# Exact softmax with a pass for the maxima against online softmax in blocks, in a cross-attention kernel

## The reference

```python
qh = (q @ wq + bq).reshape(b, -1, 16, 32).transpose(0, 2, 1, 3)     # 128 queries
kh = (k @ wk + bk).reshape(b, -1, 16, 32).transpose(0, 2, 1, 3)     # 2048 keys
vh = (v @ wv + bv).reshape(b, -1, 16, 32).transpose(0, 2, 1, 3)
score = softmax(einsum('bhqd,bhkd->bhqk', qh, kh) / 32 ** 0.5, axis=-1)
out = einsum('bhqk,bhkd->bhqd', score, vh)                          # then @ wo + bo, + x
```

## Time and profile before

| | |
|---|---|
| median of 3 runs | 3335.28 us (3335.01 to 3337.17) |
| profiled execution: span | 3332.6 us |
| TensorE busy | 3315.3 us |
| VectorE busy | 2431.5 us |
| GpSimd busy | 2110.4 us |
| ScalarE busy | 1300.5 us |
| TensorE items of this stage (line 101, two groups) | 770.9 and 743.7 us |

### The profile page before, as it was taken

The page is one execution under the profiler, slowest core; times in us unless marked ns, Lnnn a source line. Parts: engine busy times, 40 slices in busy tenths (PEclk is TensorE's granted clock), DMA queues, the critical chain, the costliest instruction groups (busy, mean ns, idle before and its releaser), DMA issues.

```text
span 3332.6 us, 81287 instructions
## 1 busy us (share of the span) xinstructions
PE 3315.3 (99%) x32145; PEld 2661.9 (80%) x32145; DVE 2431.5 (73%) x3790; ACT 1300.5 (39%) x1809; POOL 2110.4 (63%) x1537
## 2 busy tenths in 40 slices
PE   9999999999999999999999999999999999999999
PEld 6777777777777777777777777778888888888888
DVE  6566676666766766677676676767887688789997
ACT  3244444444444444444444444454213322321111
POOL 3277978879788798797987979862555000033332
PEclk9999999999999999999999999999999999999999
DMA  4111111111121111111111111122122423310000
GB/s 166 60 39 49 40 52 58 37 52 39 49 58 40 52 38 51 58 40 49 46 46 56 39 52 52 43 81 77 64 99 102 137 83 108 129 66 20 25 19 19
DMA packets 211351, 199.06 MB, mean 60 GB/s; under 512 B 11520, under 2 KB 168560, under 8 KB 209520
## 3 DMA queue, kind: packets, MB, share of 16 engines
q1 hardware_dynamic: 211056, 194.50, 18.5%
HBM read 156.32 MB, written 38.13 MB: 58 GB/s over the span
## 4 chain that ended last, share of the span: by engine, by line
PE 96%; DVE 3%; issue 0%; POOL 0%; ACT 0%; DMA 0%; SPq 0%; DVEq 0%; POOLq 0%
PE a_bank L101 70%; PE a_bank L1725 7%; PE a_bank L1697 7%; PE a_bank L1688 6%; PE a_bank L790 1%; PE a_bank L1677 1%; PE a_bank L2723 1%; PE a_bank L801 0%; PE a_bank L865 0%; PE a_bank L1713 0%; PE a_bank L1744 0%; PE a_bank L839 0%; PE a_bank L2696 0%; PE a_bank L1737 0%; PE a_bank L2219 0%
## 5 line engine op out<-in xcount | busy, mean ns | idle before, releaser
L1473 DVE TENSOR_REDUCE x_maxima<-a_bank 128x1 f32<-128x512 f32 x960 | 616.3, 684 | 331.0 <-PE a_bank L1688 331.0
L1344 ACT ACTIVATE x_probsT<-x_probsT 128x1024 f32<-128x1024 f32 x480 | 509.2, 1061 | 810.1 <-DVE x_probsT L1484 810.1
L101 PE MATMUL a_bank<-x_ctx,x_wk 128*128 128x512 f32 x3072 | 770.9, 400 | 0.0
L101 PE MATMUL a_bank<-x_wv,x_ctx 128*128 128x512 f32 x3072 | 743.7, 391 | 0.0
L101 PEld LDWEIGHTS a_bank<-x_ctx,x_wk 128*128 128x128 f32 x3072 | 557.7, 188 | 157.3 <-issue 32.6
L101 PEld LDWEIGHTS a_bank<-x_wv,x_ctx 128*128 128x128 f32 x3072 | 573.2, 188 | 130.4 <-ACT x_v L1326 5.4
L1484 DVE TENSOR_TENSOR x_probsT<-a_bank,x_shift_all 128x1024 f32<-128x1024 f32 x480 | 583.4, 1216 | 2.0 <-PE a_bank L1697 1.7
L1047 POOL TENSOR_TENSOR x_pairs<-x_probsT 128x1024 f32<-128x1024 f32 x240 | 576.7, 2403 | 12.9 <-ACT x_probsT L1344 10.8
L1238 POOL TENSOR_TENSOR x_ctx<-x_tile_raw,x_one 128x512 fp32r<-128x512 f32 x236 | 245.3, 1039 | 294.3 <-PE a_bank L101 292.7
L1510 DVE SCALAR_TENSOR_TENSOR x_k<-a_bank,x_bk,x_k 128x512 fp32r<-128x512 f32 x240 | 180.2, 751 | 305.7 <-ACT x_k L1333 305.7
L1240 POOL TENSOR_TENSOR x_ctx<-x_tile_raw,x_ctx 128x512 fp32r<-128x512 f32 x236 | 301.6, 1278 | 18.5
(11 more groups left out here) (224 smaller groups left out, 4458.1 us busy)
## 6 DMA issues: line engine op xcount, KB each, us to landing
x_tile_raw<-in_ctx SPq DMA_DIRECT2D x236, 256.0 KB, 3.1
x_shift_all<-shifts SPq DMA_DIRECT2D x60, 256.0 KB, 3.6
m_ff_src<-in_w_ff SPq DMA_DIRECT2D x44, 192.0 KB, 2.5
wq_ff<-m_ff_dst SPq DMA_DIRECT2D x44, 192.0 KB, 1.8
attT<-x_out SPq DMA_DIRECT2D x32, 256.0 KB, 2.0
s_attT<-attT SPq DMA_DIRECT2D x16, 512.0 KB, 4.2
m_w_raw<-in_w SPq DMA_DIRECT2D x32, 256.0 KB, 3.0
f_w_in<-wq_ff SPq DMA_DIRECT2D x22, 256.0 KB, 3.4
```

The source lines that it names most:

```text
L101: mm = pe.matmul(out, lhs[a], rhs[b], start=first and n == 0, stop=last and n == 2)
L1344: act.activation(half, half, ACT.Exp).then_inc(exped, 1)
L1473: dve.tensor_reduce(maxima[:, c, g * HG + j:g * HG + j + 1], banks[:, j], AX.X, ALU.max).then_inc(maxed, 1)
```

## The change

Softmax becomes online. The batch is cut into 8 blocks: 2 halves of the keys (8 tiles of 128) by 4 head groups; 128 blocks in all, counted through (`Block`, `run_blocks`: a loop body of 24 blocks). There is no `top`, no second computation of the scores and no maxima a batch ahead. Instead, for each block:

- TensorE computes the scores in two halves of 4 tiles; ScalarE copies each half out of banks 0 to 3 into one of three SBUF buffers (`keep_scores`, two copies of 1024 columns for each half).
- VectorE folds the 8 tiles of a block into one by a maximum over tiles (`fold`, twice, for two heads each); TensorE turns the four results (`turn_folds`), VectorE takes the maximum over the free axis (`shift_columns`), TensorE turns that into rows (`turn_shift`), ScalarE copies them (`keep_shift`), SP saves and loads them broadcast.
- One block later ScalarE puts the table of shifts into a PSUM bank (`make_table`), VectorE adds it to the scores in SBUF (`add_shift`, four times), ScalarE takes exp (twice 2048 columns). Two blocks later TensorE weights, three blocks later it sums the denominators (`sum_up`, one for each block). For the second half of the keys the sums so far are first scaled by exp of the drop of the maximum (`ease` on GpSimd).
- Items are made 3 blocks ahead, four in a block, all copied once (no low part of the keys is needed).

More of the change, by code:

```diff
@@ L318, with __init__, ahead, back @@
 UNROLL = 4
+PER_BATCH = 8
+RING = 3
+PERIOD = PER_BATCH * RING
+BLOCKS = B * PER_BATCH
+class Block:
+    def __init__(self, n, k):
+        self.n, self.k = n, k
+        self.group, self.half, self.at = k % HG, k % PER_BATCH // HG, k % PER_BATCH
+        self.turn = k // PER_BATCH
+    def ahead(self, d):
+        return Block(self.n + (self.k + d) // PERIOD, (self.k + d) % PERIOD)
+    def back(self, d):
+        return self.ahead(-d)
+    def count(self, per=1, plus=0):
+        return self.n * (PERIOD * per) + (self.k * per + plus)
+    def batch(self):
+        return self.n * RING + self.turn if isinstance(self.n, int) else None
+    def batches(self, per=1, plus=0):
+        return self.n * (RING * per) + (self.turn * per + plus)
+    def seconds(self, per=1, plus=0):
+        return self.n * (PERIOD // 2 * per) + ((self.turn * HG + self.group) * per + plus)
+    def ring(self):
+        return self.k % RING
+    def number(self):
+        return self.n * PERIOD + self.k if isinstance(self.n, int) else None
+    def exists(self):
+        return not isinstance(self.n, int) or 0 <= self.number() < BLOCKS
+    def from_end(self):
+        return self.number() - BLOCKS if isinstance(self.n, int) else -BLOCKS
+def run_blocks(nc, eng, step, until):
+    for k in range(PERIOD):
+        step(Block(0, k))
+    with looped(nc, eng, 1, BLOCKS // PERIOD) as n:
+        for k in range(PERIOD):
+            step(Block(n, k))
+    for k in range(BLOCKS // PERIOD * PERIOD, until):
+        step(Block(k // PERIOD, k % PERIOD))
 class Tile:
@@ L1458, in _ @@
+            for c in range(2):
+                late.weights_hi(act, 4, c)
             late.scalar(act)
@@ L1695, in score @@
+            def score(s, h):
+                c = 2 * s.half + h
+                g = s.group
+                if s.half == 0 and h == 0 and g % 2 == 0:
+                    pe.wait_ge(q_loaded[g // 2], START + s.batches(16, 16))
+                pe.wait_ge(k_ready, START + s.batches(KT, c * DC + g + 1))
+                if h:
+                    pe.wait_ge(kept, START + s.count(HG, 2))
+                elif s.back(1).exists():
+                    pe.wait_ge(kept, START + s.count(HG))
                 for t in range(TPC):
@@ L1810, in back, with weigh @@
[L1810 to L1814 removed]
+            def weigh(s, e):
+                pe.wait_ge(exped, START + e.count(2, 2))
+                if e.group == 0:
+                    pe.wait_ge(v_ready, START + e.batches(KT, BLOCK_TILES * (e.half + 1)))
+                last = s.back(1)
+                pe.wait_ge(shift_kept, START + (last.count(1, 1) if last.exists() else BLOCKS))
+                if last.half:
+                    pe.wait_ge(drop_kept, START + (last.seconds(1, 1) if last.exists() else B * HG))
+                if s.from_end() == -ITEMS_AHEAD:
+                    pe.wait_ge(k_ready, START + B * KT)
+                for t in range(BLOCK_TILES):
+                    for j in range(HG):
+                        mm = pe.matmul(bank[rows(j), misc_bank(s), 0:S],
+                                       v_t[:, e.half * BLOCK_TILES + t, cols(e.group * HG + j, DH)],
+                                       scores_of(e)[:, j, t], start=t == 0, stop=t == BLOCK_TILES - 1)
+                mm.then_inc(pv_done, 1)
@@ new lines, in _, with end_step, end_turns @@
+            for g in range(2):
+                pe.wait_ge(v_ready, START + g + 3)
+                key_item(Block(0, 2), g, 6 + g)
+            q.project(pe, 2)
+            q.turn(pe, 3)
+            for v in range(2):
+                pe.wait_ge(k_ready, START + v + 5)
+                value_item(Block(0, 2), v, 6 + v)
+            q.project(pe, 3)
+            run_blocks(nc, pe, step, BLOCKS - ITEMS_AHEAD)
+            def end_step(k):
+                step(Block(k // PERIOD, k % PERIOD))
+            def end_turns(k):
+                s = Block(k // PERIOD, k % PERIOD)
+                turn_folds(s)
+                turn_shift(s)
```

1226 lines of the change are left out of this document (482 added, 744 removed).

## The result

The changed kernel takes 4058.1 us (median of four runs, 4047.4 to 4070.4) against 3336.1 us (3335.0 to 3337.2) for the kernel before on the same chip: ratio 1.2165, 95% interval 1.2134 to 1.2195. The forecast was 3873 us with a range up to 4040: the right direction, and 185 us too little.

What follows compares the result with a forecast made beforehand. TensorE's own work bounds the kernel before; a block becomes 16.6 us of work plus 4.55 of waiting, against 17.17. Start 96, blocks 2644, last three 76 and rest 1053.6 give 3870, predicted 3873 us; range 3490 to 4040.

Steps and rivals of the forecast that it cites:

- granted clock at full: Sign expected in the profile after: TensorE's granted clock stays at full despite the two pauses in a block.
- The clock falls: Rival: work after TensorE's long pause runs at 1.2 GHz, 3.4 us more per block, 4300 us; one in eight, 50; chance 0.05.
- The wait before `turn_folds`: TensorE, free at 14.5 us in the block round, waits 3.0 us for two folds on VectorE ending at 17.5.
- The fold: VectorE's stepped maximum over 2048 elements: 3.75 us, between 2.29 (contiguous) and 4.35 (full element price).
- The wait before `weigh`: TensorE waits 1.5 us for the exponential's second half, which stands behind `keep_shift` on ScalarE.
- The moved key item: Key item ahead of score half 1 on TensorE: hides that half's wait for the first copies, and buys only this.
- The shifts through memory: Save and load of the shift row: first two `add_shift` end 2 us before the folds can start, costing nothing.
- Start and tail: Block 0 starts at 96 us; the last three blocks, without items, take 76 us.
- The rest of the kernel: After the blocks the kernel goes on as the kernel before does from 2279.0 us: 1053.6 us.
- The faster rival: TensorE hides both waits: round of 16.6 us, 3300 us in all, turning point at a round of 16.9; chance 0.06.
- The likeliest part of the range: Both waits with a fold of 3.2 to 4.35 us: 3740 to 4040 us, chance 0.71.
- the signs the prediction asked for: TensorE near 80% busy, fold 3.3 to 4.35 us, block 21 us, waits of 3 and 1.5 us, clock full.

Runs made afterwards that it cites:

- e2: Kernel as changed plus ten unneeded 512-column matmuls per block on TensorE, right before the wait of `turn_folds`; 3902.7 us.
- e7: Kernel as changed with `turn_folds` moved ahead of the second key item of a block on TensorE; 4470.4 us.
- e1: Kernel as changed with the two folds reading the same scores in storage order, so the output is not the reference's; 3498.6 us.
- e8: e4 plus the ten matmuls before the wait of `turn_folds`; 3878.7 us.
- e10: Kernel as changed with seven tile comparisons replacing the folds, second-half exponential ahead of `keep_shift`, and `add_shift` 3 ahead of `shift_columns`; 3308.4 us, ratio 0.9917 to the kernel before.
- e6: Kernel as changed with the second half of the scores put back ahead of the first key item, on TensorE alone; 4216.4 us.
- e11: e10 with the second half of the scores put back ahead of the first key item on TensorE; 3911.2 us.
- e12: e2 with the row of shifts loaded twice in sequence, the second load waiting for the first; 4218.5 us.
- e4: Kernel as changed with the exponential of the second half ahead of `keep_shift` on ScalarE; 3943.3 us.
- e5: e4 with `add_shift` 3 also moved ahead of `shift_columns` on VectorE; 3943.1 us.

## Why the prediction was right or wrong, point by point

The sum, term by term, against the profiled executions of the kernel as changed and of e2, in which the clock is nearly full:

| us | forecast | as changed | e2 |
|---|---|---|---|
| block 0 starts | 96 | 103.4 | 102.0 |
| blocks 0 to 124 | 2644 | 2775.8 | 2634.5 |
| last three blocks | 76 | 101.3 | 101.3 |
| from there to the end | 1053.6 | 1066.1 | 1066.1 |
| sum | 3870 | 4046.6 | 3903.9 |

- *The step that failed* is the term that the sum doesn't have: the forecast put the loss by the clock at nothing ("granted clock at full") and gave *The clock falls* a chance of 0.05. In the runs this term is 141 of the 177 us in the table, and 155 us by the medians of the kernel as changed and of e2 (the profiled execution lay 10 us below its median). I had the mechanism, its place and a price for one event, 3.4 us; the highest that the trace shows is 0.4 in the turns and 2.3 to 2.5 in the item, and the mean over all blocks 0.10 and 1.16. What was wrong above all is how often: "if one in eight did, 50". Of the 125 value items behind the turns 85 took 3.9 us or more, two in three. The only row on it spoke for a clock at the lower level, and no row spoke against; I had no row of TensorE pausing inside the loop, and took the absence for evidence. TensorE: Matmul & The Clock Gate of the Trainium skill, in HAM oscillation, describes a loop in which each wait starts the next work cold. The trace agrees in kind, with a granted clock of 0.942 and an item of 5.32 us in place of 3.01, but not in every round: 40 of the 125 items behind the pause kept their 3.0 us.
- *The wait before `turn_folds`*, 3.0 us: 3.10 measured. In the mean over the blocks the folds start 9.9 us after `turn_shift` (forecast 10.0) and end at 17.4 (17.35). Right, and e7 shows its working: 2.86 less work ahead of the turns gave 2.55 more of pause.
- *The fold*, 3.75 between 2.29 and 4.35: 3.81. The choice was right though its reason was thin, so the closeness is in part luck: the two prices it stood between, 3.3 and 4.35, have their middle at 3.83, not at 3.75. e1 settles what the prediction left open: the excess, 1.53 us for 2048 elements or 0.75 ns each, belongs to the step, since eight elements per output in storage order cost nothing more. The small-step rows of lines 1515 and 1522 had 1.0 ns of excess for each. The Vector Engine (DVE) Microarchitecture Reference of the Trainium skill, section 5.2, gives full rate for adjacent words and 1.73 ns per column for one hopping source, measured on programs with two sources. The trace agrees in kind: the fold's 3.81 us are 1.86 ns per column, e1's 2.28 us are 1.11, both with the fixed cost in them. The prediction says that this figure would put the time within 10 us of its own; by its own sums (3.67 for 3.75, two folds in each of 125 blocks) it is 20.
- *The wait before `weigh`*, 1.5 us: 1.67 in the block shown, 178 us in all, 1.4 a block. Right. That it stands behind `keep_shift` is right only in part: with the exponential first and a full clock (e8) 104 of 178 us stay, because `add_shift` 3 stands behind `shift_columns`. I had named only the first of two orders that hold it; it takes both (e10: 9 us).
- *The moved key item "buys only" a hidden copy*: wrong. In e6 the copy needed almost no hiding (0.15 us a block), and putting the item back costs 158 us through ScalarE's order; where comparisons stand there too the item's place is worth 603 us (e11).
- *The shifts through memory*, about 2 us spare: 1.84 us of idle time before the folds. Right, and e12 shows that what exceeds it is paid.
- *Start and tail* were 6 to 7 and 25 us too short, at either clock. At the start TensorE waited 3.82 us for `q_y` at 41.5, which I had not allowed for. In the tail I took each of the last blocks as a round without its items. But with no items TensorE waits 8.8, 8.8 and 15.2 us for folds and twice some 8 us for Pool's sum (kernel as changed):

```profile
2894.35 1.11 PE L1664 MATMUL a_bank<-x_id,x_folds 128*128 128x128 f32 x4 [8.81 <-DVE x_folds L1483]
...
2941.31 1.11 PE L1664 MATMUL a_bank<-x_id,x_folds 128*128 128x128 f32 x4 [15.23 <-DVE x_folds L1483]
...
2970.39 0.65 PE L1654 MATMUL a_bank<-x_total,x_ones 128*32 128x128 f32 x8 [8.31 <-POOL x_total L1275]
```

- *The rest of the kernel* takes 12 to 13 us more than in the kernel before, in the kernel as changed, in e2 and in e10. Its first 36 products take 10.9 us in e10 where they took 8.49; they too follow a pause. Behind them TensorE waits 8.6 us for VectorE's `s_phi_k` where it waited 0.3, and this is most of it.
- *The faster rival* had 3300 us at a round of 16.6, and its turning point against the kernel before at 16.9. e10 reaches 3308 us, but at a round of 16.34: start, tail and rest took 1267 us where the rival had 1220 for them. With them as measured the kernel before is matched at a round of about 16.5, not 16.9. And it takes another fold and two other orders than the change has.
- *The likeliest part of the range*: with a fold of 3.25 us the prediction names a round of 20.3 and 3760 us. By its own steps, 0.5 us less for each of two folds, it is 20.15 and 3750.
- Among the signs the prediction asked for, most came: a busy share of 80% in the middle (500 to 2500 us), the fold, both waits at their sizes, none elsewhere of note in the loop. The releaser before `weigh` is the exponential; before `turn_folds` the profile names a fold for 66 of 423 us and no releaser for 357. "Granted clock at full" failed, and a round of 21 us with it. With the clock restored (e2) the round is 21.14 us against 21.15.

## What to carry to other kernels

When a change puts a pause into a loop whose TensorE had none, price the clock with it: look at the item behind each pause, and set a case for it that covers most rounds, not one in eight. A cheap test is to fill the pause with products that nobody needs; if the kernel gets faster by more work and the granted clock comes back, it was the clock. A maximum over tiles read with a large step is better made as a running comparison of whole tiles, and a step moved on one engine must be moved in the order of the engine that consumes it. Removed waits don't add up while something slow lies beside them: the same reordering was worth 115 us beside a slow item and 24 us without it.

## What the runs showed of the hardware that I had not expected

- Pauses of 2.45 to 5.7 us in the loop were followed by transposes, scores or items that ran at 1.2 GHz for a part or all of their time. The item behind was over 4 us in half of the blocks of e12, in six of ten of the kernel as changed, and in nearly all of e4, e6 and e7 (granted clock 0.958, 0.942 and 0.90 to 0.92); behind the pauses of 1.1 to 1.7 us before `weigh` the weighting took its usual 1.96 us in all but one block of the kernel as changed. The share of slow items rose when the short pause was removed (e4, e5). What decides is open.
- Work added in a pause made the kernel 155 us faster (e2), 3.8%.
- A stepped maximum costs 1.67 times the contiguous one at equal elements and outputs (3.81 and 2.28 us), with the other engines unchanged.
